# Up projection of exact integers in two passes, and half of the down blocks added up by an accumulating DMA

## What is computed

```python
x = x + attn(cond(x, cond_128, fside))            # conv, 32-head attention, output projection
x = x + ffn(cond2(x, cond_128))                   # mixing over 8 experts, then this:
def ffn(x):                                       # x: 1024 tokens x 512
    gate_proj = (gate_w - rep(gate_z)) * rep(gate_s)     # 512 x 1792, int weights and zeros 0..15,
    up_proj   = (up_w   - rep(up_z))   * rep(up_s)       # one scale per group of 128 rows and column
    down_proj = (down_w - rep(down_z)) * rep(down_s)     # 1792 x 512, same
    return (silu(x @ gate_proj) * (x @ up_proj)) @ down_proj
```

## Time and profile before

| | us |
|---|---|
| median of three runs | 694.09 |
| the profiled execution's own time | 693.69 |
| its span | 691.7 |
| PE busy | 677.2 (98%) |
| DVE busy | 550.2 (80%) |
| POOL busy | 469.0 (68%) |
| ACT busy | 425.6 (62%) |

### The profile page before, as it was taken

How to read it: one execution, slowest core, us unless ns; L and a number is a source line. 1 busy time by engine, 2 the same in 40 slices (tenths; PEclk the granted TensorE clock), 3 DMA queues, 4 the chain that set the end, 5 groups by cost and what they waited for, 6 DMA issues and landing times.

```text
span 691.7 us, 14557 instructions
## 1 busy us (share of the span) xinstructions
PE 677.2 (98%) x5054; PEld 399.4 (58%) x5054; DVE 550.2 (80%) x828; ACT 425.6 (62%) x1272; POOL 469.0 (68%) x383
## 2 busy tenths in 40 slices
PE   9999999999999999999999999999989999999996
PEld 8766555656656566565655656566535555555553
DVE  4978878869869788886977878688666998888887
ACT  0478573844746566384564738547466788777774
POOL 0468874873876496487477649737627787888885
PEclk9999999999999999999999999999999999999999
DMA  7420365587387278447537736453200010000001
GB/s 253 183 92 2 124 151 126 129 215 102 98 166 189 84 152 228 107 88 239 103 97 158 199 92 152 123 122 64 33 1 1 4 28 17 17 33 30 1 0 61
DMA packets 97359, 70.24 MB, mean 102 GB/s; under 512 B 79360, under 2 KB 79904, under 8 KB 95136
## 3 DMA queue, kind: packets, MB, share of 16 engines
q1 hardware_dynamic: 96880, 69.64, 40.6%
q10 hardware_dynamic: 432, 0.01, 0.0%
HBM read 51.68 MB, written 2.21 MB: 78 GB/s over the span
## 4 chain that ended last, share of the span: by engine, by line
PE 87%; POOL 5%; DVE 4%; issue 2%; ACT 1%; DVEq 0%; POOLq 0%; ACTq 0%
PE bank L625 20%; PE bank L627 20%; PE bank L626 20%; PE bank L983 4%; PE bank L984 4%; PE bank L953 3%; PE bank L954 3%; PE bank L677 2%; PE bank L968 2%; PE bank L969 2%; POOL wqlo L1995 2%; PE bank L815 1%; PE bank L772 1%; PE bank L799 1%; PE bank L787 1%
## 5 line engine op out<-in xcount | busy, mean ns | idle before, releaser
L625 PE MATMUL bank<-wohi,oThi 128*128 128x512 f16 x256 | 97.1, 379 | 2.5 <-DVE oTlo L1674 2.3
L625 PE MATMUL bank<-wqhi,cThi 128*128 128x512 f16 x256 | 97.0, 379 | 0.9 <-POOL wqlo L1995 0.6
L626 PE MATMUL bank<-wolo,oThi 128*128 128x512 f16 x256 | 97.0, 379 | 0.0
L627 PE MATMUL bank<-wohi,oTlo 128*128 128x512 f16 x256 | 97.0, 379 | 0.0
L627 PE MATMUL bank<-wqhi,cTlo 128*128 128x512 f16 x256 | 97.0, 379 | 0.0
L626 PE MATMUL bank<-wqlo,cThi 128*128 128x512 f16 x256 | 97.0, 379 | 0.0
L1124 ACT ACTIVATE qraw<-bank 128x512 f32<-128x512 f32 x64 | 37.9, 592 | 78.2 <-PE bank L627 77.6
L1682 DVE SCALAR_TENSOR_TENSOR x<-bank,ysc,x 128x512 f32<-128x512 f32 x64 | 47.6, 748 | 43.4 <-PE bank L627 43.3
L2043 POOL TENSOR_TENSOR qinv<-qms,neghalf 128x8 f32<-128x8 f32 x28 | 53.6, 1916 | 39.2 <-ACT qms L1143 39.2
L1135 ACT ACTIVATE qsq<-qraw 128x128 f32<-128x128 f32 x256 | 75.7, 301 | 1.7
L2005 POOL TENSOR_TENSOR wolo<-wor,wohi 128x512 f16<-128x512 f32 x32 | 39.7, 1262 | 49.9 <-ACT wohi L1104 49.9
(11 more groups left out here) (216 smaller groups left out, 1844.0 us busy)
## 6 DMA issues: line engine op xcount, KB each, us to landing
wqr<-in_wq SPq DMA_DIRECT2D x8, 1024.0 KB, 7.5
wor<-in_wo SPq DMA_DIRECT2D x8, 1024.0 KB, 6.1
raw<-in_gu_w SPq DMA_DIRECT2D x28, 256.0 KB, 3.1
zeros<-in_gu_z SPq DMA_DIRECT2D x28, 256.0 KB, 4.5
wkvr<-in_wkv SPq DMA_DIRECT2D x8, 512.0 KB, 7.3
srow<-in_up_s SPq DMA_DIRECT2D x14, 256.0 KB, 5.0
raw<-in_dn_w SPq DMA_DIRECT2D x14, 256.0 KB, 2.7
zeros<-in_dn_z SPq DMA_DIRECT2D x14, 256.0 KB, 3.7
```

Of the source, the lines that this page charges most:

```text
L625: mm(o, ahi, bhi, start=start and k == 0, stop=False)
L626: mm(o, ahi, blo, start=False, stop=False)
L627: last = mm(o, alo, bhi, start=False, stop=stop and k == n - 1)
```

## The change

All four up blocks become exact integers: two matmuls each, a bank each. ACT takes block 0 out of PSUM, DVE adds blocks 1, 2 and 3 one after the other. The preparation of the scaled halves (`srow`, L1694, L2068, L1191, L1699) goes, as do the factors for it. Of the down blocks, DVE keeps 0 and 2. ACT scales blocks 1 and 3 into `dprod`, now twice as wide, and for tiles 1 to 24 one accumulating DMA that POOL issues (`move_down`) adds both to the accumulators. The last three tiles keep a form near the old one.

```diff
+DIRECT = TILES - 3
-        def up_bank(n):
-            return PA[1] if n < 2 else PC[3]
-        def exact_bank(n, c):
-            return (PA[0], PB[0] if n < 2 else PA[1])[c]
+        def up_bank(n, c):
+            return (PA[0], PA[1], PB[0], PB[1] if n < 2 else PC[3])[c]
+        def down_added(n, c):
+            return 2 * n + max(n - DIRECT, 0) + (1, 0, 2, 3)[c]
+        def down_evicted(n, c):
+            return 2 * n + (c + 1) // 2 if n < DIRECT else DIRECT + n + 1
+        def down_moved(n):
+            return 16 * min(n, DIRECT - 1)
...
             # TensorE, gate(n)
                     if g == 0 and n:
                         pe.wait_ge(a_u, n)
+                    elif n and (g < 3 or n <= 2):
+                        pe.wait_ge(d_us, 3 * n - 3 + g)
...
             # TensorE, up(n)
+                for c in range(KC):
+                    if c < 3 or n < 2:
+                        pe.wait_ge(d_g if c % 2 else a_g, 2 * n + 1 + c // 2)
+                    elif n == 2:
+                        pe.wait_ge(d_y, HQ * UNITS)
+                    else:
+                        pe.wait_ge(d_us, 3 * n)
+                    o = up_bank(n, c)[:, :]
+                    mm(o, uint[:, i, c, :], fThi[:, c, tokens(half)], start=True, stop=False)
+                    mm(o, uint[:, i, c, :], fTlo[:, c, tokens(half)], start=False, stop=True).then_inc(t_u, 1)
...
             # TensorE, down(n, blocks)
+                    if c == 3:
+                        pe.wait_ge(a_dn, down_evicted(n, 1))
+                    elif c == 2:
+                        pe.wait_ge(d_dn, down_added(n, 0))
+                    elif n and c:
+                        pe.wait_ge(a_dn, down_evicted(n - 1, 3))
                     elif n:
-                        pe.wait_ge(d_dn, down_added(n - 1, c + 2))
+                        pe.wait_ge(d_dn, down_added(n - 1, 2))
...
             # ACT
-            def down_scaled(n):
+            def down_scaled(n, c):
+                act.wait_ge(t_dn, down_done(n, c))
+                if n == DIRECT + 2:
+                    act.wait_ge(p_acc, 1)
+                elif n >= 3 and c == 1:
+                    act.wait_ge(l_acc, down_moved(n - 2))
+                A(dprod[:, n % 2, c // 2, :] if n else acc[:, 0, c, :], down_bank(n, c)[:, :], ACT.Copy,
+                  scale=dscl[:, i, c:c + 1]).then_inc(a_dn, 1)
...
             for n in range(2, TILES):
+                if LAG < n <= DIRECT + LAG:
+                    down_scaled(n - LAG - 1, 3)
                 scaled(n, 0)
...
             # DVE
+            def up_added(n):
+                u = exact[:, n % 2, :]
+                for c in range(1, KC):
+                    dve.wait_ge(t_u, KC * n + c + 1)
+                    if c == 1:
+                        dve.wait_ge(a_u, n + 1)
+                    else:
+                        dve.wait_ge(d_us, 3 * n + c - 1)
+                    V.scalar_tensor_tensor(u, up_bank(n, c)[:, :], uscl[:, half, i, c:c + 1], u, ALU.mult,
+                                           ALU.add).then_inc(d_us, 1)
...
             for n in range(2, TILES):
-                if n > LAG:
-                    down_added_to(n - LAG - 1, 3)
...
             # POOL
+            def move_down(n):
+                if n:
+                    half = n // IC
+                    pool.wait_ge(a_dn, down_evicted(n, 3))
+                    if n > 1:
+                        pool.wait_ge(l_acc, down_moved(n - 1))
+                    if n == IC:
+                        pool.wait_ge(a_xT, KC)
+                    pool.dma_start(acc[:, half, :, :].rearrange("p (c k) t -> p c k t", k=2)[:, :, 1, :],
+                                   dprod[:, n % 2, :, :], accum_op=ALU.add).then_inc(l_acc, 16)
...
             for n in range(LAG, TILES):
                 if n > LAG:
                     hidden(n - 1)
-                    add_down(n - 1 - LAG)
+                    move_down(n - 1 - LAG)
                 add_part(n)
                 hidden_low(n - 1)
```

More of the change, by code:

```diff
@@ L93, in build @@
 def build(nc, x_in, xt_in, mask_in, fs_in, cond_in, cw_in, conv_in, wq_in, wkv_in, wo_in, w0_in, w1_in, w2_in, b2_in, mix_in, vec_in,
-          gu_w_in, gu_z_in, gu_s_in, up_s_in, dn_w_in, dn_z_in, dn_s_in, const_in, sel_in, out):
+          gu_w_in, gu_z_in, gu_s_in, dn_w_in, dn_z_in, dn_s_in, const_in, sel_in, out):
     ctx = ExitStack()
@@ L959, in up @@
                 if half == 0:
[L960 to L976, removed]
-                                                  fTlo[:, c, tokens(half)]) for c in range(EXACT, KC)],
-                              True, True).then_inc(t_u, 1)
+                    pe.wait_ge(d_uint, i + 1)
+                for c in range(KC):
[8 more added lines that the diff above has]
+                    mm(o, uint[:, i, c, :], fTlo[:, c, tokens(half)], start=False, stop=True).then_inc(t_u, 1)
             def down_block(n, c):
@@ L1187, in mix_out @@
                   bias=aggb[:, q:q + 1]).then_inc(a_fnat, 1)
-            def up_high(i):
-                act.wait_ge(p_umul, i + 1)
-                A(uphi[:, i, EXACT:KC, :], raw[:, 1, EXACT * P:DM].bitcast(F32).rearrange("p (c n) -> p c n", n=P), ACT.Copy,
-                  scale=upk[:, 0:1]).then_inc(a_uphi, 1)
             def keys_high(u):
@@ L1418, in _ @@
                 if n >= LAG:
[L1419 to L1420 removed]
+                    down_scaled(n - LAG, 1)
+                up_first(n)
                 if n in (2, 3):
@@ L1432, in _ @@
             hidden_high(TILES - 1)
-            down_scaled(TILES - 2)
-            act.wait_ge(t_dn, KC * (TILES - 1) + 1)
-            act.wait_ge(p_acc, TILES - 3)
-            A(dprod[:, 1, :], down_bank(TILES - 1, 1)[:, :], ACT.Copy, scale=dscl[:, IC - 1, 1:2]).then_inc(a_dn, 1)
+            down_scaled(TILES - 2, 1)
+            down_scaled(TILES - 1, 1)
         @block.vector
@@ L1715, in finish @@
                 for t in range(HQ):
-                    if t == HQ - 1 and half and 0 < kv < HKV - 1:
-                        up_low(2 * kv - 1)
-                    elif t == 2 and half and kv == HKV - 1:
-                        up_low(IC - 1)
-                    elif t == HQ - 1 and half and kv == HKV - 1:
+                    if t == HQ - 1 and half and kv == HKV - 1:
                         scores_biased(u, kv)
                         mix_max(0)
-                    if t == 2 and not half:
-                        up_low(2 * kv - 2)
                     if t == HQ - 1 and not half:
@@ L1889, in down_added_to @@
                 o = acc[:, half, c, :]
-                dve.wait_ge(t_dn, KC * n + c + 1 + (n == TILES - 1 and c == 0))
+                dve.wait_ge(t_dn, down_done(n, c))
                 if n == IC:
@@ L1893, in down_added_to @@
                 if n:
-                    if i:
+                    if c == 3 and n == DIRECT:
+                        dve.wait_ge(l_acc, down_moved(n))
+                    elif i:
                         dve.wait_ge(d_dn, down_added(n - 1, c))
@@ L1966, in _ @@
             hidden_low(TILES - 1)
-            down_added_to(TILES - 3, 3)
-            down_added_to(TILES - 2, 0)
-            down_added_to(TILES - 2, 2)
-            down_added_to(TILES - 2, 3)
+            down_added_to(DIRECT, 3)
+            for c in (0, 2, 3):
+                down_added_to(TILES - 2, c)
             for c in (0, 2, 3):
@@ L2180, in _ @@
             pool.wait_ge(d_hlo, 1)
-            add_down(TILES - 1 - LAG)
-            add_down(TILES - 2)
-            add_down(TILES - 1)
+            for n in range(DIRECT, TILES):
+                add_down(n)
 def kernel(**inputs):
```

151 lines of the change are left out of this document (46 added, 105 removed).

## The result

The changed kernel took 696.26 us (median of 6 runs, 695.13 to 697.78), the kernel before 694.00 us on the same chip (6 runs, 692.88 to 694.27). The ratio is 1.0036, 95% interval 1.0022 to 1.0050: slower by 2.3 us. The forecast was 691.9 us, a gain of 2.2.

The account below looks back on a forecast made before the run. PE was taken to bound the feed-forward tile at 5.787 us, with Loop A and Loop B next at 5.60 and 5.59. Stretches summed to -2.16 us, 693.69 to 691.5, in the runs' terms 691.9; its range 689.5 to 693.7, overall 685.5 to 705.

Parts of the forecast that it names:

- Loop A: PE's down block 0 waits for DVE's previous-tile block 2 addition, behind three chained up additions: tile of 5.60 us.
- PE's saving: Feed-forward tile: 18 fp16 passes become 16, 0.43 us less, so PE alone would allow 5.36 us per tile.
- One that waits for its own engine's previous result takes 0.79 us: DVE's chained up additions: start-to-start step of 0.79 us, against 0.67 unchained; two such steps per tile, 1.58 us.
- the stretch from 5 to 13: Eight steps between first up additions of tiles 5 and 13: 49.20 us for 48.31 before, a loss of 0.89.
- The sum: All stretches between first up additions plus the tail: -2.16 us in total, 691.9 us in the runs' terms.
- The start: Tile 0 to 4: shorter up in tile 1, and tiles 2 and 3 where PE stays the bound, -1.29 us.
- steps 16 to 18: Two transposes per tile keep PE the bound there: -0.86 us from 13.25 before.
- the tail: After the first up addition of tile 27, DVE's work with one chained addition more: +0.79 us.
- Loop B: Third up addition, POOL's hidden product, ACT's rounding and up block 0, back to the chained additions: 5.59 us.
- The DMA, 5.3 us, hidden: POOL's accumulating DMA of 512 KB, issue to landing 5.3 us, fits the 5.60 us tile by 0.3.
- too late: Rival, chance 0.31: the DMA's landing exceeds the tile and lengthens shorter tiles; 701.1 us at a landing of 6.2.
- POOL is full: Rival, chance 0.06: the DMA issue holds POOL for 2.5 us, making the tile 6.2 us, 701 us in all.

Follow-up runs that it names:

- experiment 5: The second kernel of experiment 4 with the accumulating DMA moving block 3 alone, half the bytes (result incomplete, a bound only): 685.76 us, ratio 0.9876.
- experiment 1: Changed kernel with the two waits before DVE's up additions swapped, TensorE's block count now last, all three additions: 692.96 us, ratio 0.9984.
- experiment 3: Changed kernel with down block 2 in the idle side bank in 16 tiles: 694.13 us, ratio 1.0012.
- experiment 4: First kernel: changed kernel with the edits of experiment 1 and experiment 3 together: 692.44 us, ratio 0.9984.
- experiment 5, alone: Changed kernel with only the accumulating DMA cut to block 3, half the bytes (result incomplete, a bound only): 696.01 us, ratio 1.0029.
- experiment 6: Changed kernel with the DMA off POOL; SyncE issues two plain copies for tiles 1 to 24, addition left out: 701.96 us, ratio 1.0115.
- experiment 2: Kernel before with the waits of its chained up addition swapped, TensorE's block first, DVE's own count last: 693.81 us, ratio 0.9996.
- second kernel of experiment 4: First kernel of experiment 4 plus ACT's rounding of the hidden product moved behind up block 0: 691.72 us, ratio 0.9962.
- experiment 8: rows_low moved behind DVE's addition of down block 2: in the changed kernel 694.75 us; in the second kernel of experiment 4 692.42 us.

## Why the prediction was wrong

The mechanism was right and a term of its sum too small: the length of Loop A. Step by step:

- **PE's saving, 0.43 us to 5.36.** Right. With everything else out of the way the tile is 5.36 us (experiment 5).
- **The tile is set by Loop A, not by PE.** Right in place and order: block 0 waits for DVE's addition of block 2 behind the three up additions. The change lengthened a chain on DVE that goes through a shared bank, and PE's saving became waiting: the plain tile is 0.48 us over PE's 5.36, where 0.24 was forecast.
- **"One that waits for its own engine's previous result takes 0.79 us."** This is the step that failed. 0.79 is the time of an addition whose own count is waited for first; the changed kernel waits for it last, and then it takes 0.855. Two such steps are 1.71 us for 1.58. I had read the code's waits for what they wait for, and not for their order.
- **The rest of Loop A's sum.** Measured against forecast it is 2.57 for 2.50, 1.71 for 1.58, 0.66 for 0.67, 0.74 for 0.75 and 0.15 for 0.10: 5.83 for 5.60. So the chained steps are 0.13 of the 0.23. 0.07 more is PE, whose first pass behind a wait takes 0.31 us: I had counted running steps of 0.235 in a loop that makes PE wait. 0.05 is the handover from DVE to PE, for which I had taken the one from ACT to DVE. Each of these is small, and none was measured where it was used.
- **The 5.63 of experiment 1 is luck in part.** It lies near 5.60 because two things cancel that the forecast did not have: PE's 0.07, and 0.07 that the edit gains at the first addition, which the kernel before never had. With the chained steps alone at 0.785 the measured terms give 5.69. In the same way the stretch from 5 to 13 comes to 49.17 us there, where 49.20 were forecast, if its one step of 9.20 is counted as the usual 6.60.
- **The sum.** 0.2 us more in each of some 20 steps turns -2.16 into +2.46. Experiment 1 gives back 3.3 us of these 4.6. Its profile has one step of 9.20 for 6.60 (last section) and one of 7.56 for 6.76 in which DVE waited 0.98 us for a landing. With these two at their usual length its stretches sum to about -1.75 against the kernel before, within 0.4 of the forecast. How many of its other runs have such stalls no trace shows. The start (-1.28 for -1.29), steps 16 to 18 (-0.59 for -0.86) and the tail (+0.85 for +0.79) were near. I had given 0.05 us of error in the loop 1.1 us of time, and the real error was more than four times that; the chance of "slower" lay nearly all with the DMA, the wrong cause.
- **Loop B, 5.59.** Right as a mechanism and, like Loop A, short by its two chained steps, 0.13 of the 0.17 (experiment 3: 5.76).
- **The DMA, 5.3 us, hidden.** Right, but for the changed tile of 5.84: the DMA's landing is 5.0 us, and where POOL waits for it the issues are 5.53 us apart (experiment 4), 0.3 under that tile. That is 0.2 over my 5.3, and in the tile of 5.60 that I forecast it would have been hidden by less than 0.1. What I left out is that it is not always 5.0. The rival "too late" falls for the changed kernel (experiment 5, alone) and holds for any kernel with a faster tile. The estimate of 4.4 us for the landing, from the Trainium skill's "DMA: Bandwidth & Descriptors" (Anatomy of one DMA) and "Collectives: The Full Stack" (The bandwidth ceiling), was 0.6 short.
- **The rival "POOL is full".** It falls with experiment 6. The Trainium skill's "SBUF — State Buffer" (Who interferes with whom) speaks of a descriptor write held back by DVE's two-port mode; the issues here stand 0.77 us ahead of the next instruction in every plain tile, beside DVE instructions that read PSUM, and show no such hold.

## What to carry over

Before you take work off the engine that is busiest, write down each loop that closes through a shared buffer, with all handovers; if one is within a few per cent of the tile, the saving turns into a wait, and lengthening that loop makes it a loss. Take the price of a chained instruction only from one with the same waits in the same order, and that of an engine in the loop from where it has waited too. In the code, write the wait that is fulfilled last in time first, and the one long fulfilled behind it. Opening one loop shows the next: with the waits in the cheap order Loop A (5.63), Loop B (5.55, worked out), the DMA (5.53), PE (5.36), so a single edit could not give more than the distance to the second.

## What was not expected of the hardware

**The order of two waits costs 0.07 us.** DVE's chained additions stood 0.785 us apart with its own count waited for first and 0.855 with it last, in every plain tile of experiment 1 and of the changed kernel, and 0.78 and 0.84 in experiment 2. The handover from ACT to DVE went from 0.10 to 0.04 us by the same order, and a wait for PE's late block from 1.00 to 0.94. What the sequencer does in between no row shows.

**Some landings are up to 1.6 us late, each beside an instruction packet.** Of the second kernel of experiment 4, first 636.5 to 644 us with a late landing, then 644 to 649.5 us with a usual one: the transfer rate in 40 slices, the queues and the DMA's row.

```profile
GB/s 0 0 0 0 0 0 0 0 0 0 0 240 164 208 175 197 175 186 186 164 164 218 186 175 197 131 22 11 11 11 11 22 11 11 11 0 0 0 0 0
q0 software_dynamic: 272, 0.52, 40.7%
q8 instruction: 1, 0.02, 1.5%
acc<-dprod POOLq DMA_DIRECT2D x1, 512.0 KB, 6.6
```

```profile
GB/s 0 0 0 0 0 0 0 0 0 0 0 0 15 209 209 194 194 194 164 209 209 194 179 179 194 209 179 194 179 194 209 194 119 0 0 0 0 0 0 0
q0 software_dynamic: 272, 0.52, 55.4%
acc<-dprod POOLq DMA_DIRECT2D x1, 512.0 KB, 5.0
```

In the first, most of the bytes are through at the same rate, and then a trickle of 11 GB/s goes on for 1.7 us, about a sixteenth of the rate before, as if one of the 16 engines were behind. The one difference in the queues is one instruction packet of 0.02 MB. Past 630 us, where the transposes and loads are over, the seven profiles with 512 KB have 55 intervals from one issue to the next. In 35 no such packet falls, and none of these landings is late. In 20 one does, and 8 are late, by 0.4 to 1.6 us. So the packet alone is not enough, and when it comes may matter. That it is the cause was not tried.

**POOL's records behind an issue are long, its pace is not.** The instruction behind the issue shows 1.75 us for 1.27, yet the next one starts 1.24 us later (639.42, 640.66), as without a DMA. Only who waits for its result gets it later.

**`rows_low` waits for a POOL instruction that is already running.** Both inputs of `rows_low` lie in SBUF, while the additions of the tiles read one from PSUM. Those take 0.74 or 0.75 us whatever POOL does; `rows_low` took 0.74 us or anything from 1.06 to 2.48. The 14 profiles have 56 of them. In 42 no POOL addition or product ran at its start, and all took 0.74. In the other 14 one ran, and each `rows_low` ended 0.55 to 0.56 us after the end of a POOL instruction beside it: DVE was held until then. Started first, it holds POOL instead: POOL's product 0.16 us behind it shows 1.71 us for 1.28. Behind the down addition (experiment 8) all eight started beside a running product. In the profile of experiment 1 POOL's product ends at 575.66 and `rows_low` at 576.22:

```profile
572.72 1.73 POOL L2090 TENSOR_TENSOR hTlo<-whole,hThi 128x512 fp32r<-128x512 f32 x1
574.27 1.39 POOL L2084 TENSOR_TENSOR whole<-whole,exact 128x512 f32<-128x512 f32 x1
```

```profile
574.11 2.11 DVE L1823 SCALAR_TENSOR_TENSOR fpair<-fnat,fup,fpair 128x512 f16<-128x512 f32 x1
```

These 2.11 us left PE idle for 1.95 us, and the two windows behind had a granted clock of 0.80 and 0.63 (part of the time at 1.2 GHz, where a pass took 0.43 us a step for 0.22):

```profile
573.00:576.00 3.00, 2.08 (x10) 0.70 (x8) 2.96 (x3) 3.00 (x6) 2.66 (x3) 1.00 0.82 142
576.00:579.00 3.00, 1.97 (x8) 1.66 (x9) 2.86 (x5) 0.88 (x2) 1.91 (x2) 0.80 0.48 84
579.00:582.00 3.00, 3.00 (x11) 1.28 (x9) 0.89 (x2) 1.98 (x5) 1.78 (x2) 0.63 0.87 147
```

That step took 9.20 us for 6.6. The steps of 7.28 and 8.29 in experiment 4 also hold a long `rows_low` (2.48 and 2.45 us). Such a stall costs more than itself. That it makes the spread of the faster kernels' runs is likely and not shown, as only one run of each kernel has a trace.
